# A cross-attention and mixture-of-experts block on one core: negated maximum in one instruction, attention steps and the last expert's matmuls at other places in the queues

## The reference, cut to what matters

```python
# x: 4 x 1024 x 256; ctx: 4 x 154 x 256; mask broadcast over queries; 16 routed experts, top 8, and a shared one
x = x + xattn(layernorm(x), ctx)          # softmax(q k^T / sqrt(256), masked) v; Wq, Wk, Wv 256 x 256
x = x + ffn(layernorm(x))
# ffn: logits = l2norm(x) @ l2norm(gate_w).T ; scores = sigmoid(logits); the top 8, normalised -> combine
#      routed = sum over experts of combine_e * ((silu(x @ w_gate_e) * (x @ w_up_e)) @ w_down_e)
#      shared = (silu(x @ sw_gate) * (x @ sw_up)) @ sw_down
```

## Time and profile before

| | us |
|---|---|
| median of 3 runs | 650.99 (650.79 to 651.32) |
| the profiled execution, its own time | 650.85 |
| its span in the profile | 648.7 |
| PE busy in the span | 634.6 |
| DVE busy | 472.7 |
| POOL busy | 294.7 |
| ACT busy | 235.7 |

### The profile page before, as it was taken

How to read it: one execution, slowest core, us unless ns; L and a number is a source line. 1 busy time by engine, 2 the same in 40 slices (tenths; PEclk the granted TensorE clock), 3 DMA queues, 4 the chain that set the end, 5 groups by cost and what they waited for, 6 DMA issues and landing times.

```text
span 648.7 us, 10466 instructions
## 1 busy us (share of the span) xinstructions
PE 634.6 (98%) x3688; PEld 551.5 (85%) x3688; DVE 472.7 (73%) x941; ACT 235.7 (36%) x500; POOL 294.7 (45%) x275
## 2 busy tenths in 40 slices
PE   8898999999999999999999999999999999999997
PEld 7576888889888888888888898888888888888886
DVE  3779897868967588766868689675887768575443
ACT  5644444333243323433243332433234332432221
POOL 2517687333743356333563337433464334423333
PEclk9999899999999999999999999999999999999999
DMA  7265663424225324053244342263240531242100
GB/s 212 68 168 193 175 176 79 149 70 151 63 35 198 90 83 97 24 174 107 74 89 131 89 148 64 36 198 98 73 98 22 177 107 42 56 132 98 65 1 33
DMA packets 112655, 67.19 MB, mean 104 GB/s; under 512 B 80996, under 2 KB 102396, under 8 KB 112604
## 3 DMA queue, kind: packets, MB, share of 16 engines
q1 hardware_dynamic: 111516, 65.74, 36.0%
q10 hardware_dynamic: 1088, 0.79, 0.4%
HBM read 55.79 MB, written 10.42 MB: 102 GB/s over the span
## 4 chain that ended last, share of the span: by engine, by line
PE 91%; DVE 5%; issue 2%; ACT 1%; POOL 1%; POOLq 0%; ACTq 0%; DVEq 0%
PE y_ps L393 9%; PE gate_ps L395 9%; PE gate_ps L394 9%; PE up_ps L395 9%; PE up_ps L394 9%; PE gate_ps L393 9%; PE up_ps L393 9%; PE y_ps L394 9%; PE y_ps L395 9%; PE f_ps L538 2%; DVE hs L1155 1%; DVE W L999 1%; PE up_ps L402 1%; PE f_ps L575 1%; PE f_ps L393 1%
## 5 line engine op out<-in xcount | busy, mean ns | idle before, releaser
L1351 POOL TENSOR_TENSOR hidden<-hidden,cb 128x512 f32<-128x512 f32 x128 | 193.9, 1515 | 278.5 <-DVE hidden L1149 234.3
L866 ACT ACTIVATE hidden<-gate_ps 128x512 f32<-128x512 f32 x136 | 81.3, 598 | 292.9 <-PE gate_ps L395 292.9
L1145 DVE SCALAR_TENSOR_TENSOR hidden<-hidden,gate_ps 128x512 f32<-128x512 f32 x136 | 92.7, 681 | 102.9 <-ACT hidden L866 102.7
L393 PE MATMUL y_ps<-W,hs 128*128 128x256 f32 x544 | 154.7, 284 | 5.0 <-DVE hs L1155 5.0
L394 PE MATMUL y_ps<-W,hs 128*128 128x256 f32 x544 | 151.6, 279 | 0.0
L395 PE MATMUL y_ps<-W,hs 128*128 128x256 f32 x544 | 151.4, 278 | 0.0
L1155 DVE TENSOR_TENSOR hs<-hidden,hs 128x512 fp32r<-128x512 f32 x136 | 111.1, 817 | 21.8 <-ACT hs L873 21.6
L393 PEld LDWEIGHTS y_ps<-W,hs 128*128 128x128 f32 x544 | 102.2, 188 | 13.6 <-ACT hs L873 5.0
L393 PE MATMUL gate_ps<-xT,W 128*128 128x512 f32 x272 | 107.9, 397 | 0.0
L395 PE MATMUL gate_ps<-xT,W 128*128 128x512 f32 x272 | 107.6, 396 | 0.0
L394 PE MATMUL gate_ps<-xT,W 128*128 128x512 f32 x272 | 107.3, 395 | 0.0
(11 more groups left out here) (162 smaller groups left out, 664.0 us busy)
## 6 DMA issues: line engine op xcount, KB each, us to landing
cb<-c_rows SPq DMA_DIRECT2D x64, 512.0 KB, 4.8
blocks<-in_x_dram SPq DMA_DIRECT2D x28, 128.0 KB, 2.9
xin<-in_x_dram SPq DMA_DIRECT2D x7, 512.0 KB, 4.1
t_rows<-blocks SPq DMA_DIRECT2D x28, 128.0 KB, 2.7
xs<-t_rows SPq DMA_DIRECT2D x7, 512.0 KB, 3.5
out_dram<-x SPq DMA_DIRECT2D x7, 512.0 KB, 6.2
p_rows<-blocks SPq DMA_DIRECT2D x28, 80.0 KB, 2.3
stage<-in_L_ffn_w_gate_dram SPq DMA_DIRECT2D x16, 128.0 KB, 2.5
```

The lines of the kernel that those rows point to most:

```text
L393: mm(ps, lh, rh, start=first and i == 0, stop=False)
L866: af(ew[:, i, :], gate_ps[:, i, :], ACT.Tanh, scale=0.5).then_inc(tanh_done, 1)
L1145: V_.scalar_tensor_tensor(out=ew[:, i, :], in0=ew[:, i, :], scalar=1.0, in1=gate_ps[:, i, :], op0=ALU.add, op1=ALU.mult).then_inc(silu_don ...
L1351: pg.tensor_tensor(h[:, i, :], ew[:, i, :], cb[:, pair % PLACES, (e - 1) % 2, :], ALU.mult) \
```

## The change

1. `mask_and_max` writes the maximum with its sign turned in the reduction itself (`negate=True`); the multiplication by -1 (L1070) and the semaphore `maxes` go, and POOL's `add_bias` waits for `scaled` instead.
2. Tables: `exps` of the second half from 2 to 2.5, `swap_p` from 2.5 to 3, `add_bias` for the chunk after next from 9.5 to 12.5.
3. Pass 0, steps up to 11: `hidden_lo` and `hidden_hi` come ahead of the weight split of the step.
4. Prologue: on ACT both exponentials of chunk 0 come first, then only the tail of the values that chunk 0 needs (`vt_hi_first`); the tails of the other chunks (`write_vt_hi`) follow after the probabilities, and `t2_hi_first` comes ahead of `split_hi(3)`. On DVE likewise; `router_scaled` moves behind, and `ln2(0, 1)` ahead of `ln2_scale(0, 0)`. On PE `turn_router` moves behind `values(1)`. `move_v_tails` on SP, whose nine transfers stand ahead of the weights of expert 3, still waits for the last low part of the tails.
5. Last chunk: PE makes gate and up of expert 16 ahead of `down` of expert 13, no longer behind it.

```diff
-ACT_AT = dict(exps=(1.5, 2), probs_hi=(5,), t2_hi=(11.5,), read_z=(12.5,), tanh_scores=(13,), combine_rows=(15,))
-DVE_AT = dict(maxes=(.5, 1.5), swap_p=(2.5,), sum_reciprocal=(3.5,), probs_lo=(5,), residual=(6, 6.5),
+ACT_AT = dict(exps=(1.5, 2.5), probs_hi=(5,), t2_hi=(11.5,), read_z=(12.5,), tanh_scores=(13,), combine_rows=(15,))
+DVE_AT = dict(maxes=(.5, 1.5), swap_p=(3,), sum_reciprocal=(3.5,), probs_lo=(5,), residual=(6, 6.5),
...
-POOL_SOON = dict(add_bias=(9.5,), ln1_std=(11.5, 11.5), add_bv=(13.5, 14.5))
+POOL_SOON = dict(add_bias=(12.5,), ln1_std=(11.5, 11.5), add_bv=(13.5, 14.5))
...
             attend(0, 0)
-            turn_router()
             attend(0, 1)
             values(1, y_ps[:, 0, 0:D])
+            turn_router()
...
                 for s in range(NE):
+                    if not ahead and s + AHEAD == NE - 1:
+
+                        gate(c, NE - 1)
+                        up(c, NE - 1)
                     down(c, s)
                     if ahead:
                         front(s, c + 1)
-                    if (s + AHEAD < NE or ahead) and not (c == 0 and s == 1):
+                    if (s + AHEAD < NE - 1 or ahead) and not (c == 0 and s == 1):
...
             exps(0, 0)
-            write_vt_hi()
+            exps(0, 1)
+            vt_hi_first()
             write_v_hi(0, y_ps[:, 0, 0:D])
-            exps(0, 1)
             probs_hi_first(0)
             probs_hi_first(1)
+            write_vt_hi()
...
-            split_hi(3)
             t2_hi_first(0)
             t2_hi_first(1)
+            split_hi(3)
...
+                    if s + 1 < NE or ahead:
+                        hidden_hi(c, s + 1)
                     if c == 0 and s + EARLY < NE:
                         split_hi(s + EARLY)
-                    if s + 1 < NE or ahead:
-                        hidden_hi(c, s + 1)
...
-                V_.tensor_reduce(rsum[:, 2 * q:2 * q + 2], att[:, 2 * q:2 * q + 2, 0:KEYS], AX_X, ALU.max) \
-                    .then_inc(maxes, 1)
-                dve.wait_ge(maxes, upto(c, 2, q + 1))
-                V_.tensor_scalar(nmax[:, 2 * q:2 * q + 2], rsum[:, 2 * q:2 * q + 2], -1.0, None, ALU.mult) \
+                V_.tensor_reduce(nmax[:, 2 * q:2 * q + 2], att[:, 2 * q:2 * q + 2, 0:KEYS], AX_X, ALU.max, negate=True) \
                     .then_inc(maxed, 1)
...
             mask_and_max(0, 1)
-            router_scaled()
-            write_vt_lo()
+            vt_lo_first()
             write_v_lo(0, y_ps[:, 0, 0:D])
             sum_reciprocal(0)
             probs_lo_first(0)
             probs_lo_first(1)
+            write_vt_lo()
+            router_scaled()
...
+                    if c == 0 and s + EARLY < NE:
+                        hidden_lo(c, s + 1)
+                        if s + EARLY not in POOL_SPLITS:
+                            split_lo(s + EARLY)
                     if ahead:
                         front(s, c + 1)
                     if c + 2 < CHUNKS:
                         soon(s, c + 2)
-                    if c == 0 and s + EARLY < NE and s + EARLY not in POOL_SPLITS:
-                        split_lo(s + EARLY)
-                    if s + 1 < NE or ahead:
+                    if (c > 0 or s + EARLY >= NE) and (s + 1 < NE or ahead):
                         hidden_lo(c, s + 1)
```

More of the change, by code:

```diff
@@ L170, in xattn_moe_kernel @@
                              "kt_read", "a_made", "a_read", "bq_spread", "brow_made", "brow_scaled", "v_made",
-                             "v_hi", "v_lo", "vt_made", "vt_split", "vt_loaded", "gate_summed", "gate_inv", "gate_scaled", "gate_turned",
+                             "v_hi", "v_lo", "vt_made", "vt0_split", "vt_split", "vt_loaded", "gate_summed", "gate_inv", "gate_scaled", "gate_turned",
                              "gate_split", "keep_set", "pads_set", "bias_first", "w_hi", "w_lo_dve", "w_lo_pool"))
-        (ln1_stats, ln1_rstd, x_swapped, p_swapped, x2_swapped, t1_turned, t1_read, bias_added, x_biased, scored, scaled, maxes, maxed, exped,
+        (ln1_stats, ln1_rstd, x_swapped, p_swapped, x2_swapped, t1_turned, t1_read, bias_added, x_biased, scored, scaled, maxed, exped,
          rsummed, p_turned, p_hi, p_lo, attended, x2_made, ln2_stats, ln2_rstd, inv_norms, ln2_done, t2_turned, t2_hi,
@@ L178, in xattn_moe_kernel @@
             sem(n) for n in ("ln1_stats", "ln1_rstd", "x_swapped", "p_swapped", "x2_swapped", "t1_turned", "t1_read", "bias_added", "x_biased", "scored",
-                             "scaled", "maxes", "maxed", "exped", "rsummed", "p_turned", "p_hi", "p_lo", "attended",
+                             "scaled", "maxed", "exped", "rsummed", "p_turned", "p_hi", "p_lo", "attended",
                              "x2_made", "ln2_stats", "ln2_rstd", "inv_norms", "ln2_done", "t2_turned", "t2_hi",
@@ L311, in move_v_tails @@
             def move_v_tails():
-                sp.wait_ge(vt_split, 4)
+                sp.wait_ge(vt_split, 2)
                 for row, part in ((0, HI), (PAD, HI), (2 * PAD, LO)):
@@ L489, in values @@
                     pe.wait_ge(v_lo, 1)
-                    pe.wait_ge(vt_split, 4)
+                    pe.wait_ge(vt_split, 2)
                 elif b == 2:
@@ L773, in write_v_hi, with vt_hi_first @@
                 af(V[:, b, HI, :], ps, ACT.Copy).then_inc(v_hi, 1)
-            def write_vt_hi():
+            def vt_hi_first():
                 act.wait_ge(vt_made, 1)
@@ L779, in write_vt_hi @@
                     ins = af(Vtail[row:row + PAD, 0, :], y_ps[0:PAD, 0, D:2 * D], ACT.Copy)
-                ins.then_inc(vt_split, 1)
+                ins.then_inc(vt0_split, 1)
+            def write_vt_hi():
+                act.wait_ge(v_lo, 1)
                 af(vt[:, HI, :], y_ps[:, 0, D:2 * D], ACT.Copy).then_inc(vt_split, 1)
@@ L971, in mean_wq, with vt_lo_first, write_vt_lo @@
                 V_.tensor_scalar(wq_sum[:, KD:2 * KD], wq_sum[:, 0:KD], -1.0 / D, None, ALU.mult).then_inc(wq_mean, 1)
-            def write_vt_lo():
-                dve.wait_ge(vt_split, 2)
+            def vt_lo_first():
+                dve.wait_ge(vt0_split, 1)
                 dve.wait_ge(v_hi, 1)
                 V_.tensor_tensor(Vtail[2 * PAD:STACK, 0, :], y_ps[0:PAD, 0, D:2 * D], Vtail[0:PAD, 0, :].bitcast(F32),
-                                 ALU.subtract).then_inc(vt_split, 1)
+                                 ALU.subtract).then_inc(vt0_split, 1)
+            def write_vt_lo():
+                dve.wait_ge(vt_split, 1)
                 V_.tensor_tensor(vt[:, LO, :], y_ps[:, 0, D:2 * D], vt[:, HI, :].bitcast(F32), ALU.subtract) \
@@ L1074, in sum_reciprocal @@
                 dve.wait_ge(exped, upto(c, TILES, TILES))
-                dve.wait_ge(maxed, upto(c, 2, 2))
                 V_.reciprocal(rsum, esum).then_inc(rsummed, 1)
@@ L1220, in _ @@
             residual(0, 1)
+            ln2(0, 1)
             ln2_scale(0, 0)
-            ln2(0, 1)
             ln2_scale(0, 1)
@@ L1297, in add_bias @@
             def add_bias(c):
-                pool.wait_ge(maxes, upto(c - 1, 2, 2))
+                pool.wait_ge(scaled, upto(c - 1, 2, 2))
                 if c == 1:
```

2 lines of the change are left out of this document (1 added, 1 removed).

## The result

| | before | after |
|---|---|---|
| median, us | 650.89 (650.11 to 652.28, 6 runs) | 663.23 (661.67 to 664.49, 6 runs) |
| ratio | | 1.0187 (95%: 1.0170 to 1.0204) |
| span of the profiled execution | 648.7 | 661.0 |

12.3 us slower, where 5.9 had been forecast (656.8, range 650.8 to 660.5). In the changed file DVE's lines stand 7 further down (the low parts are L1087 and L1089, `swap_p` L1044, `hidden_lo` L1162), ACT's too (L835 and L880), PE's at the same numbers.

A forecast was written before the change was run, and what follows sets the result against it. PE was taken as the bound, busy nearly throughout, with almost no waits from 110 us on. 650.85 + 5.0 + 2.0 - 1.1 = 656.75, with the 0.14 to the median about 656.8 us; range 650.8 to 660.5.

The forecast's parts named there:

- part 2: Prologue and chunk 0, up to `down(10)` of pass 0: gains first, then losses, +2.0 us in all; bounds -2.5 and +4.5.
- Part 1: Chunks 2 to 7: `swap_p` half a step later makes PE wait at each `attend`, +5.0 us; bounds 3 and 6.5.
- The 2.15 estimated from the Trainium skill: Chunks 2 to 7: alternative landing time in us for the small second load, making the late swap cost about 2.6 us.
- the upper bound with 3.0: Chunks 2 to 7: if loads land in 3.0 us, the longest seen, the late swap costs 6.5 us.
- Part 2, first item: Prologue, router's turn: ACT reaches its copy about 1.0 us earlier, so PE gains 1.0, not 3, and idles 2 us.
- `down(2)` is 1.3 and `down(3)` 3.5 earlier: Chunk 0: `hidden_lo` ahead of splits and two fewer multiplications; the 2.1 us wait and the slow clock behind it go.
- `swap_p` [ends] 63.5 to 65.4, I take 64.5: Chunk 1's `swap_p`, 64.58 before; the chain behind it makes `attend` -0.3 to +1.5 us late, taken as +1.5.
- PE idles before that `attend` ... +1.5: Ahead of chunk 1's `attend`: PE idles longer than 2.1 us, so its clock falls, costing +1.5 us.
- `add_bias` away from `hidden_lo(10)`: -0.9: Pass 0: `hidden_lo(10)` took 1.89 us in place of .7 and PE waited 0.9; moving `add_bias` gains that, -0.9.
- Part 3: Last chunk: gate and up of expert 16 come one `down` earlier, -1.1 us; bounds 0.9 and 1.4.
- Part 4: Multiplications in chunks 2 to 7 and `add_bias` at 12.5 in passes 1 to 5: nothing; other bound 0.4 each.
- the rival: Logits: `write_t2_lo` held by `add_bias` makes PE wait, five passes at 0.4 us, total 660.3; chance 0.13.

The follow-up runs named there:

- b_prologue: The kernel before with only the new prologue order on PE, ACT and DVE and the negated maximum; ratio to before 0.9993.
- a_warm: The changed kernel with unread matmuls on PE, 50 ahead of `attend(1,0)` and 16 ahead of `down(10)` of pass 0; ratio to before 1.0154.
- a_lt6: The changed kernel with the new order in pass 0 for steps 0 to 5 alone; ratio to before 1.0134.
- a_s7: The changed kernel with the old order at step 7 of pass 0 alone; ratio to before 1.0150.
- a_s8: The changed kernel with the old order at step 8 of pass 0 alone; ratio to before 1.0136.
- b_end: The kernel before with only gate and up of expert 16 ahead of `down(13)` in the last chunk; ratio to before 0.9974.
- a_pass0: The changed kernel with the old order in pass 0, the late swap kept; ratio to before 1.0069.
- a_lt5: The changed kernel with the new order in pass 0 for steps 0 to 4 alone; ratio to before 1.0095.
- c_z: The changed kernel with early swap, new pass 0 order for steps 0 to 4 alone, and `read_z` ahead of splits 3 and 4; ratio to before 0.9991.
- c_zold_b: c_zold timed a second time; ratio to before 0.9916.
- c_best1: The changed kernel with `swap_p` at 2.5, exponentials at 2, and the new pass 0 order for steps 0 to 4 alone; ratio to before 0.9978.
- a_swap: The changed kernel with `swap_p` back at 2.5 and the second exponentials at 2; ratio to before 1.0049.
- b_zend: The kernel before with `read_z` ahead of the splits of experts 3 and 4, and the last expert's edit; ratio to before 0.9979.
- c_zold: The changed kernel with early swap, pass 0 order wholly old, and `read_z` ahead of the splits of experts 3 and 4; ratio to before 0.9926.

## Where the prediction was right and which steps failed

The direction was right. 6.4 us were missed, all of them in part 2, which was put at +2.0 and measured some 8.5. Two of its steps failed. The idle time at the router's turn was seen but its price was put at nothing, and the new order of pass 0 was followed only as far as `attend(1,0)`, so that the wait at `down(10)` and the slow clock behind it were missed.

- **Part 1, +5.0: right mechanism, 4.5 measured** (six places, L1089, ACT idling 1.9, the swap late). For chunk 4 the working gave 0.90 and the trace 0.53. The difference is the landing: 2.9 was read from before, here it is 313.20 - 310.63 = 2.57. That the total fits is partly luck: chunk 3, forecast as the largest, came 0.50 late for 1.35, and chunk 7, forecast as the smallest, 1.04 for 0.35. From `swap_p` to the second load it took 6.14 us in chunk 3 and 6.57 in chunk 7, where the kernel before had 6.86 and 6.16, and the working carried those over. The six starts together are 4.0 late for the forecast 5.0, and the slower first matmul, which was not in the sum, adds 0.5. The 2.15 estimated from the Trainium skill, "DMA: Bandwidth & Descriptors", Anatomy of one DMA, for its GpSimd path is too short for these loads: 2.57 in chunk 4, 3.08 in chunk 1. The rows decided rightly. Redone for all six chunks, landings of 2.15 would give 2.3 and not 2.6, and the upper bound with 3.0 is 7.4 and not 6.5. Nor is the sum exact: 656.75 and the 0.14 are 656.9.
- **Part 2, first item, "PE gains 1.0, not 3, and idles 2 us": failed.** The idle time was right to a tenth (1.96), and then I let its consequence go. The clock falls behind it (0.50 at 38 to 40 us), `down(0)` starts at 45.92 in place of 45.15, and the gain of 1.0 is a loss of 0.8. I had charged exactly this for the other wait, three items further down. b_prologue shows it alone.
- **"`down(2)` is 1.3 and `down(3)` 3.5 earlier": 1.5 too much each.** `down(2)` starts at 57.15 (56.92 before), `down(3)` at 61.44 (63.44), about the 1.8 of the item above. The wait of 2.1 and the slow clock behind it did go.
- **"`swap_p` [ends] 63.5 to 65.4, I take 64.5": it ended at 66.46.** 1.8 of the 2.0 are the item above. What follows the swap was right: 8.0 to ACT's start (8.1 forecast), `hidden_lo(6)` ahead, the split of expert 10 holding the second low part. From 66.46 the same chain gives 81.0, and PE started at 80.55. So `attend(1,0)` is +3.1 and not +1.5.
- **"PE idles before that `attend` ... +1.5": right,** 1.9 us by a_warm.
- **"`add_bias` away from `hidden_lo(10)`: -0.9": right by itself, wrong in this kernel.** The seven kernels with `add_bias` at 12.5 and the old order from step 6 or earlier on show no wait at `down(10)`, and the five with it at 9.5 and the old order, the kernel before among them, show 0.9. But I stopped following the new order at `attend(1,0)`. At steps 7 and 8 it puts the second layer norm behind `hidden_lo`, and `down(10)` waits 2.7 in place of 0.9. In the profiled execution the clock falls a third time behind that. By the table of stretches this is +1.8 for the wait and, of the 2.3 behind `down(10)`, some 1.7 for the clock. Together with the forecast -0.9 the term was 4.4 us off. a_lt6, a_s7 and a_s8 show the wait; a fall of the clock behind it is seen in the changed kernel's trace alone.
- **Part 3, -1.1: right.** 0.9 in the table, 1.18 in b_end, and `down(16)` without a wait.
- **Part 4, nothing: right** for chunks 2 to 7, which have no wait but at `attend`. a_pass0, a_lt6, a_lt5, c_z and c_zold_b have one of 0.8 at the logits in pass 0. It is not the one of the rival: in a_pass0 the second `write_t2_lo` is held by POOL's product (from 106.64), and `add_bias` starts later, at 107.95.

The sum with measured terms: 4.5 + 3.1 + 1.9 + 1.8 + 1.7 - 0.9 = 12.1, against 12.3. The upper bound for part 2, +4.5, had no room for a second and third fall of the clock, nor for a new wait behind `attend`.

Several of my expectations behind the prediction failed as well: that the late swap alone would delay `attend(1,0)`, that the old order at step 7 would leave the clock falling, that c_best1 and c_z would be 2.5 us or more faster than before (1.4 and 0.6, the latter not clear of noise), and that the new order in steps 0 to 4 would cost nothing.

## What to carry to other kernels

On an engine that is busy nearly all the time, a term that moves a wait isn't finished until every idle stretch that it makes is priced twice, once for itself and once for the slower clock behind it. When an order is changed in a loop, follow every iteration that it touches: here `down(4)` came 3.7 us earlier (65.56 for 69.22), which was all lost at the next `attend`, and steps 5, 7 and 8 cost, where an instruction that isn't needed yet, or waits, now stands ahead of one that is. And a part that gains nothing alone (an earlier prologue, an earlier copy) may be one half of a gain: look at which queue holds the next thing back.

## What the runs showed of the hardware

- Behind idle stretches of about 2 us PE's clock fell in some traces and not in others: at the turn it fell behind 1.96, 2.21 and 2.47, and stayed up behind 1.80 (a_swap) and 1.99 (a_lt6). At `down(3)` it fell behind 2.06 in the kernel before and stayed up behind 2.06 in b_zend and 2.16 in b_end. At `down(10)` it fell behind 2.69 in the changed kernel and stayed up behind 2.69 in a_swap and 2.78 in b_pass0. So in this case the idle time alone doesn't tell.
- Executions of one kernel differ by more than the effect of some of the edits. In c_zold the mean clock tells them apart (645.2 to 646.5 at 1.0, 647.7 to 648.2 at 0.997). In b_end it doesn't: those at 0.997 lie between 649.8 and 655.3.
- PE kept busy with useless matmuls during a wait keeps its clock (a_warm), which gave 2.2 us back, barely clear of noise.
- The idle time in the bracket of a matmul understates what a short wait costs, by about 0.25 us here (316.54 in the changed kernel: 0.16 in the modelled end of the matmul ahead, 0.08 in the first one behind).
